# Last stage: values, mask and scores moved to the head of TensorE's step

## The reference, cut to what matters

```python
for i in range(DEPTH):
    x = attn_layer(shift_tokens(x), Wqkv[i], q_scale[i], k_scale[i], Wo[i]) + x
    x = ffn_layer(shift_tokens(x), ln_g[i], ln_b[i], W1[i], b1[i], W2[i], b2[i]) + x

def attn_layer(x, Wqkv, qs, ksc, Wo):
    q, k, v = split(x @ Wqkv)                    # 3 x 1024 columns, 16 heads
    q, k = l2norm(q) * qs, l2norm(k) * ksc
    q = q * cos * scale + rotate_half(q) * sin * scale
    k = k * cos / scale + rotate_half(k) * sin / scale
    return local_attention(q, k, v) @ Wo         # mask, softmax, values in windows of 32

def ffn_layer(x, ...):                           # layer norm, a * gelu(gate), back to 128
```

## Time and profile before

| | |
|---|---|
| median of 3 runs | 2900.07 us (2897.07 to 2904.63) |
| profiled execution, its own time | 2894.76 us |
| its span, first to last instruction | 2892.6 us |
| mean granted TensorE clock | 0.940 |
| busy: PE, DVE, ACT, POOL | 2589.2 (90%), 1775.8 (61%), 1536.8 (53%), 1363.5 (47%) |
| first and last score matmul of the last stage | 1826.1 and 2849.8 us |

### The profile page before, as it was taken

One profiled execution on the slowest core, in us unless ns is written; L12 is line 12 of the kernel. 1 busy time (PEld: TensorE's weight loads), 2 busy tenths in 40 slices (PEclk: granted clock), 3 DMA queues, 4 the chain that ended last, 5 costly groups with the idle time before them and its releaser, 6 DMA issues. The chain is left out here.

```text
span 2892.6 us, 56780 instructions
## 1 busy us (share of the span) xinstructions
PE 2589.2 (90%) x20009; PEld 1658.0 (57%) x20009; DVE 1775.8 (61%) x4074; ACT 1536.8 (53%) x4979; POOL 1363.5 (47%) x1981
## 2 busy tenths in 40 slices
PE   6999978898989979867499997899999999999997
PEld 3555545555646646545345554466666666666665
DVE  4566655545657745554645554777777777777773
ACT  1455535524747736532135553566666666666664
POOL 0444434302536614300014443877777777777772
PEclk8899988999989989988679998999999999999998
DMA  2000000010000000000000001010010101011000
GB/s 69 1 1 1 1 8 2 12 33 5 2 4 2 2 33 1 6 1 8 22 6 1 1 1 51 20 34 20 21 36 27 34 23 31 23 31 34 20 25 7
DMA packets 45706, 47.77 MB, mean 17 GB/s; under 512 B 11947, under 2 KB 31413, under 8 KB 45430
## 3 DMA queue, kind: packets, MB, share of 16 engines
q1 hardware_dynamic: 45430, 44.18, 5.5%
HBM read 31.05 MB, written 0.52 MB: 11 GB/s over the span
## 5 line engine op out<-in xcount | busy, mean ns | idle before, releaser
L1033 DVE TENSOR_REDUCE negmax<-scores 128x1 f32<-128x508 f32 (+4 forms) x512 | 212.5, 467 | 215.1 <-PE scores L918 183.9
L2272 ACT ACTIVATE net_probs<-bank,net_negmax 128x96 f32<-128x96 f32 x768 | 250.9, 339 | 172.8 <-DVE net_negmax L2408 172.6
L1013 POOL TENSOR_TENSOR l_xattn_probs<-l_xattn_probs,rowinv 128x512 f32<-128x512 f32 x128 | 130.3, 1039 | 421.3 <-DVE rowinv L1025 421.3
L1013 POOL TENSOR_TENSOR lora_probs<-lora_probs,rowinv 128x508 f32<-128x508 f32 (+1 forms) x256 | 149.5, 617 | 246.5 <-DVE rowinv L1025 246.5
L2334 POOL TENSOR_TENSOR net_probs<-net_probs,net_inverse 128x384 f32<-128x384 f32 x192 | 158.7, 827 | 216.8 <-DVE net_inverse L2404 216.8
L2408 DVE TENSOR_REDUCE net_negmax<-bank 128x4 f32<-128x384 f32 x192 | 106.3, 554 | 245.1 <-PE bank L2107 244.4
L2326 POOL TENSOR_TENSOR net_rope<-net_rope,net_sin_parts 128x512 f32<-128x512 f32 x192 | 244.0, 1271 | 7.6 <-DVE net_sin_parts L2378 7.6
L2347 POOL TENSOR_TENSOR net_rope<-net_rope,net_head_inv 128x512 f32<-128x512 f32 x192 | 201.2, 1048 | 7.5 <-POOL net_head_inv L1880 0.9
L124 DVE COPY turned<-flip 128x512 f32<-128x512 f32 (+3 forms) x280 | 163.0, 582 | 64.5 <-PE flip L945 52.6
L918 PE MATMUL scores<-kT,qM 64*128 64x512 f32 (+2 forms) x768 | 191.3, 575 | 5.9 <-ACT kT L122 2.4
L739 DVE TENSOR_REDUCE negmax<-scores 128x2 f32<-128x256 f32 (+2 forms) x192 | 157.6, 822 | 62.2 <-PE scores L647 35.5
(11 more groups left out here) (434 smaller groups left out, 6535.1 us busy)
## 6 DMA issues: line engine op xcount, KB each, us to landing
net_w_qkv<-in_L_ffn_Wqkv SPq DMA_DIRECT2D x12, 768.0 KB, 5.7
net_vals_between<-net_vals SPq DMA_DIRECT2D x48, 192.0 KB, 2.5
net_w_out<-in_L_ffn_Wo SPq DMA_DIRECT2D x6, 512.0 KB, 4.2
net_vals_between<-net_vals SPq DMA_DIRECT2D x48, 64.0 KB, 2.0
moe_w<-in_L_ffn_w13T SPq DMA_DIRECT2D x8, 256.0 KB, 2.8
net_w<-in_L_ffn_W SPq DMA_DIRECT2D x6, 341.0 KB
moe_w<-in_L_ffn_w2T SPq DMA_DIRECT2D x8, 128.0 KB, 2.3
ctx_tok<-in_ctx SPq DMA_DIRECT2D x1, 768.0 KB, 6.6
```

Of the source, the lines that this page charges most:

```text
L1013: last = nc.gpsimd.tensor_tensor(own, own, rowinv[:, u * tail + w:u * tail + w + 1].to_broadcast([P, k1 - k0]), ALU.mult)
L1033: last = nc.vector.tensor_reduce(negmax[:, u * tail + w:u * tail + w + 1], scores[:, 2 * qt + h, k0:k1], AX.X, ALU.max, negate=True)
L2272: last = nc.scalar.activation(prob_blocks(g)[:, w, :], score_blocks(g)[:, w, :], ACT.Exp, bias=maxima[:, g % 4, w:w + 1], accum_out=sums[: ...
```

## The change

On TensorE the values of group s-3 and then mask and scores of group s come first in the step, then the projections, then turn, flip and side work. The values keep their group number: those of group s-3, which ended step s, now begin it. The value projection waits for `stored` of one group more, that of this step's values, and ScalarE's copy of the heads, still the first thing in ScalarE's step, takes group s-3 and no longer s-4. Nothing else is edited; VectorE, GpSimd and SyncE keep their queues.

```diff
                     for s in TICKS:
-                        u = at_tick(s, PROJ, 2, S)
-                        ...      (query, key and value projection)
-                            until(pe, stored, min(G, s - VALUES))
-                            until(pe, v_copied, u)
-                            nc.tensor.matmul(v_bank, own, ...).then_inc(v_filled.sem, 1)
-                            values_in = u + 1
+                        g = s - VALUES
+                        if 0 <= g < G:
+                            m, c = group(g)
+                            pe.wait_ge(moved.sem, moved.at(0, g + 1))
+                            if c % 4 == 0:
+                                j = g // 4
+                                pe.wait_ge(mid_in[j % 4].sem, mid_in[j % 4].at(j // 4, 2))
+                            until(pe, stored, g)
+                            until(pe, v_copied, values_in)
+                            ...  (12 value matmuls, the last signals summed)
                         g = s
                         if 0 <= g < G:
                             ...  (mask and scores)
                             last.then_inc(scored.sem, 1)
+                        u = at_tick(s, PROJ, 2, S)
+                        ...      (query, key and value projection)
+                            until(pe, stored, min(G, s - VALUES + 1))
+                            until(pe, v_copied, u)
+                            nc.tensor.matmul(v_bank, own, ...).then_inc(v_filled.sem, 1)
+                            values_in = u + 1
                         g = s + TURN
                         ...      (turn, flip, side work)
-                        g = s - VALUES
-                        ...      (the same waits and 12 value matmuls)
@@ ScalarE
                     for s in TICKS:
-                        g = s - VALUES - 1
+                        g = s - VALUES
                         if 0 <= g < G:
                             act.wait_ge(summed.sem, summed.at(0, g + 1))
                             copy("act", rope[:, m % 3, :, 0, cols_of(c)], heads...).then_inc(stored.sem, 1)
```

More of the change, by code:

```diff
@@ L2067, in _ @@
                     for s in TICKS:
+                        g = s - VALUES
[7 more added lines that the diff above has]
+                            until(pe, v_copied, values_in)
+                            given = flat_p[:, g % 3, :].rearrange("p (w h q) -> p w h q", w=BLOCKS, h=2)
+                            for w0, w1_, own in ((0, 2, vals[:, m % 3, 0, :]), (2, 3, mid[:, m % 2, :]), (3, 4, vals[:, m % 3, 1, :])):
+                                for h in range(2):
+                                    last = nc.tensor.matmul(heads[rows_of(h), w0 * QB:w1_ * QB], own[:, c * D + h * DH:c * D + (h + 1) * DH],
+                                                            given[:, w0:w1_, h, :], start=True, stop=True)
+                            last.then_inc(summed.sem, 1)
+                        g = s
+                        if 0 <= g < G:
+                            until_copied(pe, g)
+                            until(pe, exped, g - 1)
+                            nc.tensor.matmul(score_bank(g), ident16[:, :], window16[:, :], start=True, stop=False)
+                            for w in range(BLOCKS):
+                                k0 = max(0, w * QB - WINDOW)
+                                first = w * KEYS + (WINDOW if w == 0 else 0)
+                                for h in range(2):
+                                    last = nc.tensor.matmul(bank[rows_of(h), 4 + g % 2, first:(w + 1) * KEYS],
+                                                            qk_T[rows_of(h), g % 2, 0, w * QB:(w + 1) * QB],
+                                                            qk_T[rows_of(h), g % 2, 1, k0:(w + 1) * QB],
+                                                            start=False, stop=(w == BLOCKS - 1))
+                            last.then_inc(scored.sem, 1)
                         u = at_tick(s, PROJ, 2, S)
@@ L2096, in _ @@
                             values_in = u + 1
[L2097 to L2111, removed]
                         g = s + TURN
```

## The result

The changed kernel takes 2985.53 us (median of 4) against 2900.92 us (median of 4): ratio 1.0296, 95% interval 1.027 to 1.0322. It is slower by 85 us; the forecast was 2996. The profiled execution took 2988.71 us, span 2986.6 us.

A forecast was written before the change was run, and what follows sets the result against it. TensorE bounded the stage; the new order closes a chain longer than its work in most steps. Jobs of 47.40 instead of 43.34 us, over 23 jobs 93 us, plus 3, give 2996 us, range 2950 to 3045.

The forecast's parts named there:

- (a): Value projection on TensorE comes 1.63 us later, so its 31.9 us stall on ScalarE's heads copy goes: at most -32 us.
- (b): Values at the head of the step need VectorE's copy of the flip, queued behind both products; only side work lies between.
- (c): Projection starts only after the scores, so squares and VectorE's products come late, closing a chain of 5.38 us.
- the closed chain: Mask to next mask through scores, projection, square, two products, copy of the flip and values: 5.38 us per step.
- Odd steps over ScalarE: Second chain in odd steps: value projection, its copy, four exponentials, copy of q and k: 5.47 us.
- Layer normalization at nothing: VectorE's row chain ending step 5 costs nothing: step 6's reduce ends at 2.77, just ahead of the products at 2.84.
- The sum: 47.40 - 43.34 = 4.06 us per job, 93 us over 23 jobs, plus 3 us in the eight steps behind.
- The signs: Profile signs: values wait some 90 us, VectorE for squares about 190, little for scores; jobs 47.4 us, clock 1.00.
- In time: Rival: the flip's copy arrives in time, only the removed stall counts: 2868 us, at most about 2857; chance 6%.
- no change: Rival: a chain of about 4.7 us in six steps leaves the job at 43.34 us; chance 5%.
- The clock rival: TensorE's clock falls to 1.2 GHz, 2.6 us more per step; in a quarter of steps +120 us, about 3115; 6%.
- The rule that I weighed: Skill rule: stopping TensorE shortly and repeatedly can swing its clock; the forecast kept 1.00, with gaps of at most 1.8 us.

The follow-up runs named there:

- e4: Kernel before with only the value projection moved behind the scores in odd steps: 2894.09 us, ratio 0.9991.
- e8: Kernel before with the value projection behind the scores and ScalarE's two scalings of step 7 ahead of the squares: 2871.43 us, ratio 0.9911.
- e3: Changed kernel with VectorE's two products moved behind its copies of the flip and of q and k: 2931.96 us, ratio 1.0119.
- e5: Changed kernel with one more VectorE product of the same size ahead of the two, into a tile nobody reads: 3082.99 us, ratio 1.0654.
- e1: Kernel before with mask and scores alone moved ahead of the projections, values left at the end of the step: 2986.16 us, ratio 1.0316.
- e2: Changed kernel with mask and scores put back behind the projections, values left at the head of the step: 2995.5 us, ratio 1.0335.

## Why the prediction was right, point by point

*(a) The stall removed.* Right: it is gone. What its removal is worth without the rest is not the 32 us that the prediction gave as the most, but nothing measurable (e4), until a second edit on ScalarE is made (e8).

*(b) and (c), the closed chain.* Right, and the step shown above has it link by link. e3 (a link taken out of it) and e5 (one link longer, at the undisturbed clock) moved the even steps by about what the chain gives, except step 2 in both. The prediction put the values into it as its last link; e1 shows that they are dispensable. Copy of the flip and values end together with the copy of q and k (5.38 and 5.37 in the prediction), so either is enough to close it. Part (c) alone, the scores ahead of the projection, thus gives the whole loss. Part (b) alone gives one of the same size too, but over another chain, with the reduce in it (e2); so the two do not add up.

*Odd steps over ScalarE.* Right in their length: 5.47 forecast and measured in step 1; steps 5 and 7 with their additions 5.67 and 6.23 for 5.77 and 6.34.

*Layer normalization at nothing.* Right: step 6 takes 5.36, as step 0 does. The spare, 0.07 in the forecast, is used up already (the reduce ends at 2339.60, the products start at 2339.55), and in e5, with one product more, step 6 takes 6.22 and not 5.96.

*The sum.* Two terms were mis-sized, with opposite signs. The difference of a job was forecast as 47.40 - 43.34 = 4.06; it is 46.77 - 43.58 = 3.19. Two things made it too large. I added whole durations where the next operation starts earlier (flip 0.49 for 0.44, output projection 3.74 for 3.66, scalings 0.87 for 0.76), and I took the period before from a mean over 22 jobs, whose last interval is short: 21 of them are 43.58 and the last is 38.33, as it ends in steps that have no projection any more. Against that the stage's first 16 steps lost 18.3 us (from 78.13 to 96.43 us from mask to mask), over twice the 8.1 that two jobs had in the sum. That the total came out close is in part luck, since the two misses nearly cancel.

The start loses more for two reasons. Its first output projection comes only at 1883.26, so TensorE had less work of its own there: steps 0, 1, 2 and 5 took 3.7 to 4.2 us before, well under the chain, and take 6.2 to 7.1 after. And the granted clock, 0.95 over these 16 steps before, is 0.91 after, with five falls in the first ten steps, behind idle stretches of 1.7 to 3.1 us. I estimate this at up to 5 us of the 18.3: (1 - 0.91) * 96.4 less (1 - 0.95) * 78.1.

The profiled pair differs by 94 us of span: 18.3 for the first 16 steps, 65.7 for the 20 jobs (1.7 of it one fall of the clock), 3.9 for the next job, 0.8 for the rest, and 5.2 us by which the stages ahead of it, which the change doesn't touch, took longer in this execution. The stage itself thus lost 89 us where the sum had 96.

*The signs.* Right: the period (46.8 for 47.4), the values' wait (90 forecast, 87.7) in steps 6, 2 and 0 above all and none of it in steps 3 and 4, the clock near 1.00 from 1900 us on. Wrong in size: VectorE's wait for squares is 132 us and not 190, and its wait for scores did not fall to little but to 118. VectorE idles at the reduce, and for 29.2 us at the reciprocal, where I had all its idle time at the squares.

*The rivals.* "In time" and "no change" are out: the kernel is clearly slower. The clock rival is out as the main cause, since the granted clock is 1.00 over 1900 to 2900 us. But in that stretch it falls once, after the 1.52 us shown above, and the key projection behind takes this (timeline of PE):

```profile
2343.12 1.95 PE L2121 MATMUL bank<-net_w_qkv,xnT 128*128 128x512 f32 x2
```

That cost 1.7 us. In 20 jobs it fell twice in e1, six times in e2 and in 17 of them in e5. The rule that I weighed, of the Trainium skill ("TensorE: Matmul & The Clock Gate", section "A second HAM failure mode: psum-queue depth-cycling"), says that a kernel which stops TensorE often and shortly between groups of matmuls can swing between the two levels. These rows bear it out as an effect; its price in the changed kernel is small, and in e5 it is some 28 us.

## What to carry to other kernels

In a loop of steps over engines with fixed queues, busy shares do not tell what a new order costs. Look for each operation at which *other* work stands between producer and consumer, in every queue that it passes. A new order can close a chain from one step to the same place in the next, and where that chain is longer than the busiest engine's own work, its length is the period. A wait that disappears from the list says nothing yet; the same chain may end at the next consumer (e1), or its removal may need a second edit elsewhere to count (e4, e8). Take the period before from the steady middle of a stage, between the starts of the same operation, and the start of the stage for itself.

## What the runs showed of the hardware that was not expected

The granted clock fell behind idle stretches of TensorE that were no longer than others that it passed without a fall. In the 20 steady jobs of the changed kernel step 6 idles 1.52 us every time, and the fall came once (in e1 twice). In e2 it idles 1.74 us every time, and the fall came in 6 of 20 jobs. At 2.38 us (e5) it came in 17 of 20, at a cost of about 1.65 us each, and once more in a step 3. The mean granted clock of the stretch (1.00, 0.99 and 0.97) shows little of this; the lengths of the same matmul in successive jobs show it plainly.
